# Six local transformer layers: bands filled by DMA, Gelu ahead of Exp, and matmuls reordered

## The reference

```python
for i in range(6):
    x = attn_layer(shift_tokens(x), Wqkv[i], q_scale[i], k_scale[i], Wo[i]) + x
    x = ffn_layer(shift_tokens(x), ln_g[i], ln_b[i], W1[i], b1[i], W2[i], b2[i]) + x
# attn_layer: 16 heads of 64
q, k, v = split(x @ Wqkv)
q = l2norm(q) * qs;  k = l2norm(k) * ksc
q = q * cos * scale + rotate_half(q) * sin * scale       # k with 1 / scale
out = local_attention(q, k, v) @ Wo
# local_attention: windows of 32 queries see their own and the previous 32 keys
attn = softmax(where(mask, -max, (q @ k.T) * 8.0));  out = attn @ v
# ffn_layer
a, gate = split((layernorm(x) * g + b) @ W1 + b1)          # 341 + 341
return (a * gelu(gate)) @ W2 + b2
```

## Time and profile before

| | |
|---|---|
| median of 3 runs | 7142.1 us (7134.1 to 7146.59) |
| the profiled execution | 7146.77 us, its span 7144.5 us |
| busy over the span | PE 76%, PEld 46%, DVE 62%, ACT 54%, POOL 48% |
| DMA | 79753 packets, 102.01 MB |

### The profile page before, as it was taken

One profiled execution on the slowest core, in us unless ns is written; L12 is line 12 of the kernel. 1 busy time (PEld: TensorE's weight loads), 2 busy tenths in 40 slices (PEclk: granted clock), 3 DMA queues, 4 the chain that ended last, 5 costly groups with the idle time before them and its releaser, 6 DMA issues. The chain is left out here.

```text
span 7144.5 us, 148393 instructions
## 1 busy us (share of the span) xinstructions
PE 5401.0 (76%) x55030; PEld 3273.5 (46%) x55030; DVE 4401.4 (62%) x5698; ACT 3887.7 (54%) x6333; POOL 3429.4 (48%) x1391
## 2 busy tenths in 40 slices
PE   4736777087594848578888888888888888888886
PEld 3524444022121212255555555555555555555554
DVE  4352111342333424488888888888888888888885
ACT  0002222022131213278888777887778778888884
POOL 0000000000000000188888888888888888888883
PEclk8658888588796869789999999999999999999997
DMA  0000000300101010000000000000000000000001
GB/s 17 0 7 20 27 27 27 50 2 12 16 0 27 1 27 0 35 22 7 6 7 28 6 6 13 21 7 6 12 22 7 6 27 6 7 7 12 7 7 28
DMA packets 79753, 102.01 MB, mean 14 GB/s; under 512 B 16344, under 2 KB 55138, under 8 KB 77934
## 3 DMA queue, kind: packets, MB, share of 16 engines
q1 hardware_dynamic: 79632, 100.41, 6.4%
HBM read 63.67 MB, written 11.53 MB: 11 GB/s over the span
## 5 line engine op out<-in xcount | busy, mean ns | idle before, releaser
L99 POOL TENSOR_TENSOR ln_post_rstd<-ln_post_var,neg_half 128x8 f32<-128x8 f32 x16 | 26.6, 1662 | 2922.8 <-DVE ln_post_var L80 2922.8
L1591 POOL TENSOR_TENSOR d_qk_swap<-d_qk_raw,d_rot 128x512 f32<-128x512 f32 x768 | 1389.0, 1838 | 67.4 <-ACT d_qk_raw L1299 40.4
L1598 POOL TENSOR_TENSOR d_rnorm<-d_sq_clip,neg_half 128x32 f32<-128x32 f32 x192 | 1232.4, 6419 | 271.6 <-DVE d_sq_clip L1466 271.6
L834 ACT ACTIVATE c_pt<-c_ps 128x512 f32<-128x512 f32 (+1 forms) x640 | 354.5, 555 | 1118.8 <-PE c_ps L752 1116.8
L1137 PE MATMUL d_ring<-d_wqkv,d_xin 128*128 (+1 forms) x1536 | 810.2, 665 | 174.3 <-ACT d_xin L1389 169.3
L866 DVE TENSOR_REDUCE c_mx<-c_ps 128x1 f32<-128x512 f32 (+3 forms) x768 | 416.8, 556 | 772.9 <-PE c_ps L737 768.9
L1449 DVE TENSOR_TENSOR d_qk_part<-d_qk_raw,d_rot 128x1024 f32<-128x1024 f32 x384 | 597.7, 1559 | 253.6 <-ACT d_qk_raw L1299 251.0
L1575 POOL TENSOR_TENSOR d_probs_n<-d_probs,d_prec 128x1024 f32<-128x1024 f32 x192 | 545.5, 2841 | 315.8 <-DVE d_prec L1491 315.8
L1299 ACT ACTIVATE d_qk_raw<-d_ring 128x512 f32<-128x512 f32 x768 | 435.8, 594 | 453.9 <-PE d_ring L1137 450.2
L766 PE MATMUL c_ps<-c_pt,c_vg 128*32 128x512 f32 (+3 forms) x1536 | 629.3, 507 | 4.7 <-DVE c_ots L871 4.7
L1137 PEld LDWEIGHTS d_ring<-d_wqkv,d_xin 128*128 128x128 f32 x1536 | 319.7, 216 | 560.0 <-issue 449.2
(11 more groups left out here) (259 smaller groups left out, 10498.5 us busy)
## 6 DMA issues: line engine op xcount, KB each, us to landing
d_v_prev<-d_v SPq DMA_DIRECT2D x192, 128.0 KB, 2.3
b_w<-in_L_ffn_w SPq DMA_DIRECT2D x64, 256.0 KB, 3.4
d_wqkv<-in_L_ffn_Wqkv SPq DMA_DIRECT2D x6, 1536.0 KB, 8.7
c_kp<-c_k_scratch SPq DMA_DIRECT2D x30, 256.0 KB
c_qp<-c_q_scratch SPq DMA_DIRECT2D x24, 256.0 KB
d_rot<-in_rot_base SPq DMA_DIRECT2D x6, 1024.0 KB, 6.4
c_k_scratch<-c_kparts SPq DMA_DIRECT2D x5, 768.0 KB, 5.2
c_q_scratch<-c_qparts SPq DMA_DIRECT2D x4, 768.0 KB, 3.6
```

What stands on the lines that cost most here:

```text
L1591: mm = eng.tensor_tensor(qk_swap[:, which, :, out:out + hd], qk_raw[:, which, :, src:src + hd], rot[:, bass.ds(par, 1), which, 1, bass.ds( ...
L1598: eng.tensor_tensor(rnorm[:, :], sq_clip[:, :], neg_half[:, 0:2 * HEADS], ALU.pow).then_inc(rn_ready, 1)
```

## The change

1. The bands are filled by DMAs that SP issues, eight per tile of 32 partitions x 2 KB, and ScalarE's eight copies are gone. For that `band` is `[P, 4, HEADS, WIN]`, blocks of 32 tokens, and the matmul reads four pieces of 32. `band_ready` counts 128 per tile.
2. SP's list is written by slots: for each slot the eight band DMAs (wait for the transposes), then the carry of V (wait for the attention). The weight loads keep their place by slots, one or two later.
3. ScalarE, even slot: a Gelu on one column (`table_probe`), the three Gelus, and then Exp, where Exp came first.
4. ScalarE: `xin` is copied before the two V copies, after a wait for both matmuls of V.
5. VectorE, odd slot: hidden units, rope, sum and reciprocal, where the sum came first.
6. TensorE: the second feed-forward matmul behind all four projections, where it stood between the second and third; the matmuls of V ahead of those of the variance.

```diff
-        band = [sb(f"band{p}", [P, HEADS, P]) for p in range(2)]
+        band = [sb(f"band{p}", [P, 4, HEADS, WIN]) for p in range(2)]
...
-                def carry(m, p):
-                    eng.wait_ge(v_evac, 2 * (m + 1))
-                    eng.wait_ge(pv_ready, m + 1)
-                    eng.dma_start(v_prev[P - WIN:P, :], v_sb[p][P - WIN:P, :]).then_inc(v_carried, 16)
+                def slot(n, u, f, g):
+                    if f:
+                        eng.wait_ge(blocks_ready, n - 1)
+                        eng.sem_inc(passed, 1)
+                        if f == 2:
+                            eng.wait_ge(pv_ready, n - 3)
+                        for w in range(4):
+                            r = slice(32 * w, 32 * w + 32)
+                            eng.dma_start(band[u][r, w, :, :], own_t[r, :, :]).then_inc(band_ready, 16)
+                            to = band[u][32 * w - 32:32 * w, w, :, :] if w else band_prev[u][96:128, :, :]
+                            eng.dma_start(to, prev_t[r, :, :]).then_inc(band_ready, 16)
+                    if g:
+                        eng.wait_ge(pv_ready, n - 2)
+                        eng.dma_start(v_prev[P - WIN:P, :], v_sb[1 - u][P - WIN:P, :]).then_inc(v_carried, 16)
...
@@ TensorE
-                            eng.matmul(op[r:r + 64, h // 2, :], v_sb[1 - p][:, h * DH:(h + 1) * DH], band[1 - p][:, at, :],
+                            eng.matmul(op[r:r + 64, h // 2, :].rearrange("p (w t) -> p w t", t=WIN), v_sb[1 - p][:, h * DH:(h + 1) * DH], band[1 - p][:, :, at, :],
...
                         qk(0)
                         qk(1)
+                    if a:
+                        qk(2)
+                        qk(3)
                     if late:
...
                         mm.then_inc(w2_ready, 1)
-                    if a:
-                        qk(2)
-                        qk(3)
...
+                    if s:
+                        par_v = eng.snap(parity(n - 1))
+                        values(0)
+                        values(1)
                     if odd:
                         eng.wait_ge(csq_ready, k - 1)
...
                         mm.then_inc(var_done, 1)
-                    if s:
-                        par_v = eng.snap(parity(n - 1))
-                        values(0)
-                        values(1)
@@ ScalarE
                     def values():
+                        eng.wait_ge(v_ready, 2 * n)
+                        if live(-1):
+                            eng.activation(xin[1 - p][:, :], xs[:, bass.ds(eng.snap(column(n + 1)), P)], ACT.Copy).then_inc(xin_ready, 1)
                         for c in range(2):
...
-                    if u == 0:
-                        if f:
-                            bands((0, 1))
-                        if g:
-                            attended()
-                        if f:
-                            bands((2, 3))
-                    elif f:
-                        bands((0, 1, 2, 3))
+                    if g and u == 0:
+                        attended()
...
-                    if s and u == 0:
-                        exponent()
                     if even:
+                        eng.activation(table_probe[:, :], keep[:, 0:1], ACT.Gelu)
...
+                    if s and u == 0:
+                        exponent()
@@ VectorE
-                            eng.wait_ge(band_ready, n - 2)
+                            eng.wait_ge(band_ready, 128 * (n - 2))
...
-                    if f:
+                    def total():
                         eng.wait_ge(exp_ready, n - 1)
...
+                    if f and u == 0:
+                        total()
                     if late:
...
                                           ALU.mult).then_inc(rope_ready, 1)
+                    if f and u == 1:
+                        total()
                     if a:
                         cosine(0)
```

52 lines of the change are left out of this document (20 added, 32 removed).

## The result

The change is **slower**. The changed kernel takes 7312.5 us (median of 4 runs, 7306.7 to 7322.8), the kernel before 7144.4 on the same chip: ratio 1.0238, 95% interval 1.022 to 1.0256. The forecast was 7065, range 6995 to 7200. The profiled execution has a span of 7309.8 us.

What follows compares the result with a forecast made beforehand. VectorE was taken as the thread that bounds each pair: 20.95+20.25 = 41.2 us against 42.1, -84 us over some 93 pairs, with the tables' +7 -77 us; from the median 7142.1 to 7065 us, range 6995 to 7200.

Steps and rivals of the forecast that it cites:

- E: VectorE's stretch from the even slot's softmax sum to the odd slot's rope; forecast to fall from 23.85 to 20.95 us.
- O: VectorE's stretch from the odd slot's rope to the next even sum; forecast 20.25 us.
- Terms 1 and 2: Even slot: feed-forward ahead of the exponential, and earlier projections; together E shrinks by 2.9 us, the sum adding 1.5 in O.
- the late pair: Pair after a layer's tables in the trace before: VectorE came late, its multiplies had their data, E was 22.44 us.
- Is the rest ready by then?: Even slot, TensorE and ScalarE up to rope: Gelu and hidden units done 20.4 us into E, in time by 0.55.
- Term 4: Values ahead of the variance on TensorE: VectorE gets the variance later, +1.6 us in every pair.
- Term 3: Odd slot: first multiply 1.14 us without loss to GpSimd; residual add 12.4 us after rope, where it was 12.8.
- At nothing: ScalarE's band copies leaving (5.0 us per tile), their transfers, table loads and TensorE's changed layout: counted as no time.
- signs: Expected trace: E 20.9 to 21.3 us, 1.6 us variance wait, TensorE's hidden-unit wait below 1 us, ScalarE below 60% busy.
- A: Slower: on SP the carry of V queues behind the eight band transfers, delaying V copies and rope; 7195 us, chance 0.17.
- B: Slower: early projections bring nothing as GpSimd gets between the even slot's two multiplies; 7190 us, chance 0.11.
- D: Larger gain: TensorE idles less, its granted clock holds and VectorE's residual waits go; 7000 us and less, chance 0.12.

Runs made afterwards that it cites:

- b2: Kernel before with one part alone: in the even slot the input copy ahead of the values' copies on ScalarE; 7024.1 us, ratio 0.9825.
- a1: Changed kernel with the variance product back ahead of the values products on TensorE; 7086.9 us, ratio to the kernel before 0.9917.
- d3: Changed kernel with five unread products on TensorE ahead of the broadcast in each even slot; 7224.8 us, ratio to the kernel before 1.0106.
- c4: Kernel before with band transfers, early input copy and the second feed-forward product behind all four projections; 7016.5 us, ratio 0.9818.
- c1: Kernel before with bands by transfer and the early input copy, all orders as before; 7027.5 us, ratio 0.9833.
- c3: Kernel before with bands by transfer, early input copy and the odd slot's sum behind its rope; 7226.6 us, ratio 1.012.
- b1: Kernel before with the band part alone: transfers and new layout, ScalarE's band copies gone; 7093.5 us, ratio 0.9923.
- a2: Changed kernel with the even slot's attended products ahead of the broadcast on TensorE; 7271.7 us, ratio to the kernel before 1.017.
- d2: Changed kernel without the early input copy, which stands behind the values as before; 7271.2 us, ratio to the kernel before 1.0168.

## Why the prediction was wrong, step by step

43.78 measured against 41.2 forecast is 2.58 us a pair, over 93 pairs 240 us; the miss is 248. Of it 1.20 us lie in E (22.15 against 20.95), 0.73 in the usual O (20.98 against 20.25) and 0.63 in slow odd stretches. By the prediction's steps:

- **Terms 1 and 2, the value: right.** E came out at 21.0 where the clock held, forecast 20.95; b2 shows the 22.5 of the late pair, a1 the further 1.4. But the end of E hangs on two chains that are equally long: inverse norm ready 4630.64+7.44-4617.28 = 20.80 us into E, as forecast, and the Gelu, for which VectorE waits 1.59 us.
- **"Is the rest ready by then?": this step failed.** It took TensorE's durations at full clock and found 0.55 us of slack. Behind the wait for the diagonal the attended products take up to 1.93 us more, and the Gelu, with the hidden units and rope behind it, comes late by more than the slack. This is 22.15-21.0 = 1.15 us a pair; d3, which changes nothing but TensorE's idle time there, brings the mean E back to 21.20. I had read the waits of the kernel before (TensorE for the hidden units) as something that vanishes, and did not ask where TensorE, now early, would stand next.
- **Term 4, the late variance: the direct price was near (1.35 us, forecast 1.6), its consequence left out.** I put it "on VectorE itself" and stopped. It also delays GpSimd's diagonal, for which TensorE then waits. Together 226 us, of which some 125 are the direct part (92 x 1.35), already in the forecast. On its own it costs 25, on bands and early copy 151: the price depends on whether a cushion is left.
- **Term 3, the odd slot: wrong in the order of two engines.** The first multiply was to take GpSimd's and VectorE's shared access first and last 1.14 us. GpSimd's normalisation started 0.41 us ahead of it, at 4600.13, and the multiply (2.57 us) ends 1.08 us after the normalisation. The residual add comes 13.3 us after rope, forecast 12.4. With what follows, the usual O is 0.73 us over the forecast. The moves of sum and Gelu together cost 2.0 us in O (17.63 in c4, 19.63 in a1); the sum's alone, with the second feed-forward product early, 1.6 (18.02 in c1, 19.63 in c3).
- A further 0.63 us a pair are slow odd stretches (mean 21.61, usual 20.98), for which the prediction had no term: most of it is the 11 stretches of 23.87 us, in which the second multiply is 1.0 us longer and TensorE's slow attended products hold the variance by 1.6 us.
- **At nothing: right or better.** Copies, transfers and layout alone gain 52 us; with the early copy nothing (7027.5 against 7024.1).
- **The signs** of the prediction came true in part: VectorE waits 1.49 us for the variance, TensorE not at all for the hidden units, and ScalarE is busy 388 of 700 us. But E at 20.9 to 21.3 us stands in a third of the pairs only. No sign looked at TensorE's clock or at where else it would wait.
- **Rivals.** A (carry of V) did not happen in the changed kernel. Issues stand 0.63 us apart, closer to A's 0.74 than to my 0.47, and still ScalarE waited 4.2 us in all 64 pairs. But the slack is small: in three other kernels the V copies do wait for the carry (145.3 us in b1, 155.2 in a2, 219.4 in d2). B: refuted by b2. D held the mechanism that decided, TensorE's idle time and its clock, but with the wrong sign. SP's issues in order of time:

```profile
4585.57 0.59 SPq L1077 DMA_DIRECT2D d_band<-d_own_t  x1
4586.20 0.59 SPq L1079 DMA_DIRECT2D d_band<-d_prev_t  x1
```

The drain of about 1380 ns on top of a table load, which the Trainium skill states (ScalarE: Activation LUTs, What ACT_TABLE_LOAD costs), shows in no run. The loads take 1283 ns, ScalarE is idle 1.2 us in all ahead of 64 of them, and the next activation follows at once (ScalarE in order of time, changed kernel):

```profile
4635.10 1.28 ACT L1384 ACT_TABLE_LOAD   x1
4636.39 0.20 ACT L1384 ACTIVATE d_table_probe<-d_keep 128x1 f32<-128x1 f32 x1
```

The exclusive access of VectorE and GpSimd (the Trainium skill, SBUF — State Buffer, on the shared port pair) agrees with Term 3's rows: the multiply ended 1.08 us after the normalisation, about the 1.2 us that it takes undisturbed, so it got next to nothing done before. The second multiply of the slow odd stretches, 2.29 instead of 1.28 us beside GpSimd's `qk_swap`, fits the same reading; no run tests it apart.

What is shown: the order of the variance costs 226 us in the changed kernel, and unread products in TensorE's waits give back 88 and 111 us of 168. What is not: why the clock falls behind some waits of 2.37 us and not behind others, and how much of the 226 is clock; the runs bound that only by the split above. Why the second feed-forward matmuls run slow in some odd stretches and not in others is open too.

## What to carry to other kernels

When a change lets an engine run ahead, find the next thing it will wait for, and price the work behind that wait at the lower clock if the engine is TensorE: the wait itself may be free, the slow products behind it are not. A wait on VectorE can be a cushion that absorbs a delay elsewhere, or that hides an instruction (the sum); two edits that each use the same cushion do not add, so measure parts of a bundle alone and in pairs. Here one moved copy and no more gave 1.75% where the bundle lost 2.4%.

## What the runs showed of the hardware that was not expected

- Five unread products, 1.3 us of work, in each of TensorE's waits for the diagonal made the kernel 1.2% faster (7312.5 to 7224.8).
- The window from 3900 to 6700 us has a granted clock of 0.94 in the changed kernel, 0.95 before, and 1.00 in c4, whose TensorE has the same real work. It doesn't tell the time by itself: b2 has 0.97 and takes 7024.1 us, c4 7016.5, c3 0.97 and 7226.6.
- Twice the bytes (202.6 MB instead of 102.0) and eight more issues a slot on SP cost no time that shows: b1 is 52 us under the kernel before, c1 within 4 us of b2. The V copies' wait for the carry behind them is 145.3 us in b1, 21.8 before.
- A VectorE multiply of 128 x 1024 takes 1.2 us or 2.3 to 2.7 us by where it starts (GpSimd's instructions run beside it). In the odd stretches of the changed kernel a start 7.88 us after rope gave 1.2 us, a start at 7.92 gave 2.3, and 2.9 us in the whole stretch.
